# Attention layers of a graph network on one core: projection and maxima in one block instead of two

## What is computed

```python
def gat_layer(x, W, att_src, att_dst, bias, src, dst, n):
    h = (x @ W).reshape(n, 4, 32)
    a_src = einsum('nhc,hc->nh', h, att_src)
    a_dst = einsum('nhc,hc->nh', h, att_dst)
    e = leaky_relu(a_src[src] + a_dst[dst], 0.2)
    m = segment_max(e, dst, num_segments=n)
    ex = exp(e - m[dst])
    denom = segment_sum(ex, dst, num_segments=n)
    out = segment_sum((ex / denom[dst])[:, :, None] * h[src], dst, num_segments=n)
    return out.reshape(n, 128) + bias

h = elu(gat_layer(h, W1, ...)); h = elu(gat_layer(h, W2, ...))
```

## Time and profile before

| | |
|---|---|
| time, median of 3 runs | 6702.77 us (6701.74 to 6705.58) |
| the profiled execution: time / span of its trace | 6699.18 us / 6697.7 us |
| mean granted TensorE clock | 0.856 of full speed |
| TensorE matmul / weight load busy | 4445.1 us (66%) / 2524.8 us (38%) |
| VectorE busy | 3983.5 us (59%) |
| ScalarE busy | 1573.7 us (23%) |
| GpSimd busy | 1564.2 us (23%) |
| L1372, the maxima, two forms of 100 passes | 342.2 us and 342.1 us |
| L1324, the counts, 2500 passes in two layers | some 270 us of busy time in each layer |
| layer 1, first block to end of maxima | 2715.6 to 3130.7 us |
| layer 2, first block to end of maxima | 3886.5 to 4259.9 us |

### The profile page before, as it was taken

How to read it: one execution, slowest core, us unless ns; L and a number is a source line. 1 busy time by engine, 2 the same in 40 slices (tenths; PEclk the granted TensorE clock), 3 DMA queues, 4 the chain that set the end, 5 groups by cost and what they waited for, 6 DMA issues and landing times. The chain is left out here.

```text
span 6697.7 us, 52624 instructions
## 1 busy us (share of the span) xinstructions
PE 4445.1 (66%) x15996; PEld 2524.8 (38%) x15998; DVE 3983.5 (59%) x4400; ACT 1573.7 (23%) x1840; POOL 1564.2 (23%) x1634
## 2 busy tenths in 40 slices
PE   3501111337999999898888888788879887444443
PEld 1100000024554454687333378433334443333333
DVE  6412122678887786698999979899990111111112
ACT  0000000001579700444455410255540003000000
POOL 1677777100000000000000000000000001777776
PEclk9999999999999999656999965799999998555555
DMA  3001010143468606354333346333326666222222
GB/s 58 6 10 18 10 16 12 27 174 134 121 171 237 184 1 246 98 166 125 115 111 111 115 138 188 101 115 111 112 95 245 245 245 172 52 53 53 53 53 56
DMA packets 624187, 729.35 MB, mean 109 GB/s; under 512 B 96339, under 2 KB 556401, under 8 KB 604703
## 3 DMA queue, kind: packets, MB, share of 16 engines
q1 hardware_dynamic: 571790, 669.98, 32.4%
q0 software_dynamic: 52144, 56.00, 3.5%
HBM read 542.42 MB, written 183.38 MB: 108 GB/s over the span
## 5 line engine op out<-in xcount | busy, mean ns | idle before, releaser
L1080 POOL DMA_INDIRECT ring<-rel_dram,rel_pair x806 | 765.6, 950 | 4709.5 <-POOLq L68 4464.2
L878 PE MATMUL total<-to,from 128*128 128x384 f32 x2816 | 939.4, 492 | 34.3 <-issue 28.5
L1625 PE MATMUL sums<-acc,hw 128*64 128x392 f32 x2144 | 747.5, 504 | 138.0 <-DVE acc L1559 137.6
L1160 PE MATMUL total<-ring,onehot 128*128 128x128 f32 x1612 | 415.3, 439 | 579.0 <-DMA ring<-rel_dram,rel_pair 578.5
L517 POOL DMA_INDIRECT cells_dram<-rec,place x742 | 715.8, 965 | 226.1 <-issue 220.0
L686 PE MATMUL alike<-right,left 18*128 18x512 bf16 x352 | 174.4, 616 | 818.6 <-DVE top L646 662.3
L878 PEld LDWEIGHTS total<-to,from 128*128 128x128 f32 x2816 | 524.0, 190 | 450.0 <-issue 121.7
L1115 DVE TENSOR_SCALAR onehot<-iota,loc_pair 128x128 f32<-128x128 f32 x806 | 179.9, 286 | 814.8 <-PE total L1160 814.8
L1160 PEld LDWEIGHTS total<-ring,onehot 128*128 128x128 f32 x1612 | 357.2, 324 | 636.9 <-issue 636.8
L1625 PEld LDWEIGHTS sums<-acc,hw 128*64 128x64 f32 x2144 | 269.7, 138 | 581.2 <-issue 306.9
L620 DVE CAST lo_i<-rows 128x128 int32<-128x128 f32 x11 | 2.7, 244 | 714.8 <-DMA rows<-cells_dram 714.8
(11 more groups left out here) (341 smaller groups left out, 5977.6 us busy)
## 6 DMA issues: line engine op xcount, KB each, us to landing
strip<-ac_dram SPq DMA_DIRECT2D x100, 1600.0 KB, 6.5
count<-ac_dram SPq DMA_DIRECT2D x200, 784.0 KB, 4.2
ac_dram<-stage SPq DMA_DIRECT2D x625, 192.0 KB, 2.4
lo_row<-lo_dram SPq DMA_DIRECT2D x44, 1024.0 KB, 7.3
h<-ac_dram SPq DMA_DIRECT2D x26, 1600.0 KB, 8.3
acc<-ac_dram SPq DMA_DIRECT2D x24, 1600.0 KB, 8.8
rel_dram<-rows SPq DMA_DIRECT2D x25, 1024.0 KB, 5.4
mask_dram<-mask SPq DMA_DIRECT2D x25, 800.0 KB, 5.6
```

The source lines that it names most:

```text
L878: nc.tensor.matmul(spots[:, at(spot), 0:WIDTH].rearrange("p o n -> p (o n)"), from_[:, n % RING, u, :], to[:, n % RING, u, :, :].rearrange ...
L1080: pool.indirect_dma_start(ring[:, j % SLOTS, :], None, m.rel_dram[:, :], bass.IndirectOffsetOnAxis(ap=m.rel_pair[:, j:j + 1], axis=0)).the ...
L1160: last = nc.tensor.matmul(total[:, at(col, D)], onehot[:, j % U, :], ring[:, j % SLOTS, :], start=False, stop=False, skip_group_check=True)
L1625: last = nc.tensor.matmul(psum[kk * 2 * HC:(kk + 1) * 2 * HC, banks(i) + q, 0:PIECE], hw[:, t, k, :], p[n % 3][:, piece], start=t == 0, st ...
```

## The change

Both blocks of `gat_layer` become one. In it:

- SyncE issues the loads of the weight, the attention vectors and the bias and then, with no meeting of engines between, the counts of tiles 0 and 1 (in layer 2 with their masks).
- TensorE makes the 7 pieces of `hwT` (now through four banks), then the 7 spread pieces of head 0, in layer 1 the transposes of tiles 0 and 1, then the spreads of heads 1 to 3, count(0) and count(1). Only then come the 25 row tiles, four at a time into the one bank `proj`, with a wait for ScalarE's copy ahead of each next four, and the 25 score matmuls into the same bank. Tiles 2 to 24 follow as before.
- ScalarE copies the pieces of `hwT`, makes in layer 1 the marks of tile 0, copies head 0, makes mask 0, marks 1 and mask 1, copies heads 1 to 3, and then the row tiles (7 copies, which VectorE did in 25) and the scores (3 copies). Marks of tile 2 and what follows come after that.
- VectorE takes the maxima of tiles 0 and 1 head by head ((0,0), (1,0), (0,1), (1,1), ...), then tile by tile as before.
- A mask buffer is free when the last pass that reads it is done, by the list `TOPS`: for tile 0 that is the seventh pass.

The diff, cut to its core:

```diff
+    quads = [range(t, min(t + 4, NT)) for t in range(0, NT, 4)]
...
-            psum = ps("proj", [P, 8, 512])
...
-                for t in range(NT):
-                    dve.wait_ge(projected, t + 1)
-                    v.tensor_copy(hw[:, t, :, 0:HC], psum[:, 2 + t % 4, 0:D].rearrange("p (h c) -> p h c", h=HEADS)).then_inc(laid, 1)
...
-                for t in range(NT):
-                    if t >= 4:
-                        pe.wait_ge(laid, t - 3)
-                    nc.tensor.matmul(psum[:, 2 + t % 4, 0:D], m.hT[:, t * P:(t + 1) * P], w[:, :], start=True, stop=True).then_inc(projected, 1)
...
-        with phase(nc) as (sb, ps, sem, block_):
...
+            psum, sums, proj = ps("rows", [P, 4, 512]), ps("sums", [P, 512]), ps("proj", [P, 512])
...
+            TOPS = [(T, k) for k in range(HEADS) for T in range(2)] + [(T, k) for T in range(2, NT) for k in range(HEADS)]
...
                     if not first:
                         if T >= 2:
-                            sp.wait_ge(topped, HEADS * (T - 1))
+                            sp.wait_ge(topped, tops_until(T - 2))
...
+                sp.dma_start(w[:, :], weight).then_inc(w_in, 16)
...
                 load(0)
                 load(1)
...
+                pe.wait_ge(kept, len(blocks))
+                pe.wait_ge(ready, 1)
+                spread_head(0)
+                if first:
+                    turn_tile(0)
+                    turn_tile(1)
+                for k in range(1, HEADS):
+                    spread_head(k)
+                count_tile(0)
+                count_tile(1)
+                for g, tiles in enumerate(quads):
+                    if g >= 1:
+                        pe.wait_ge(laid, g)
+                    for c, t in enumerate(tiles):
+                        last = nc.tensor.matmul(proj[:, c * P:(c + 1) * P], m.hT[:, t * P:(t + 1) * P], w[:, :], start=True, stop=True)
+                    last.then_inc(projected, 1)
+                pe.wait_ge(laid, len(quads))
+                for t in range(NT):
+                    last = nc.tensor.matmul(proj[:, t * 8:t * 8 + 8], hwT[:, t * P:(t + 1) * P], att_h[:, :, :].rearrange("p k h -> p (k h)"),
+                                            start=True, stop=True)
+                last.then_inc(scored, 1)
+                for T in range(2, NT):
+                    if first:
+                        turn_tile(T)
+                    count_tile(T)
...
+                if first:
+                    mark(0)
+                keep_head(0)
+                if first:
+                    mask_tile(0)
+                    mark(1)
+                    mask_tile(1)
+                for k in range(1, HEADS):
+                    keep_head(k)
+                for g, tiles in enumerate(quads):
+                    act.wait_ge(projected, g + 1)
+                    n = len(tiles)
+                    nc.scalar.activation(hw[:, tiles[0]:tiles[0] + n, :, 0:HC], proj[:, 0:n * P].rearrange("p (t h c) -> p t h c", t=n, h=HEADS),
+                                         ACT.Copy).then_inc(laid, 1)
+                act.wait_ge(scored, 1)
...
+                if first:
+                    mark(2)
+                    for T in range(2, NT):
+                        mask_tile(T)
                         if T + 1 < NT:
                             mark(T + 1)
...
+                for i, (T, k) in enumerate(TOPS):
```

More of the change, by code:

```diff
@@ L1269, in gat_layer @@
             mask_in, col_in, out = ([sem(f"{n}{k}") for k in range(2)] for n in ("mask_in", "col_in", "out"))
-            ready, marked, turned, counted = (sem(n) for n in ("ready", "marked", "turned", "counted"))
-            d_ = sem("d")
+            w_in, att_in, d_, ready, done, kept, projected, laid, scored, noted = (
+                sem(n) for n in ("w_in", "att_in", "d", "ready", "done", "kept", "projected", "laid", "scored", "noted"))
+            marked, turned, counted = (sem(n) for n in ("marked", "turned", "counted"))
             block = block_()
-            pieces = [(k, cols) for k in range(HEADS) for cols in blocks]
             SPAN = 5
@@ L1305, in _, with spread_head, turn_tile, count_tile @@
             def _(pe):
[L1306 to L1321, removed]
+                def spread_head(k):
+                    for b, cols in enumerate(blocks):
+                        q = len(blocks) * k + b
+                        if q >= 4:
+                            pe.wait_ge(taken, q - 3)
+                        nc.tensor.matmul(psum[:, q % 4, 0:cols.stop - cols.start], att_rep[:, 0, k, :], hwT[:, cols], start=True, stop=True).then_inc(spread, 1)
+                def turn_tile(T):
+                    pe.wait_ge(marked, T + 1)
+                    for s in range(STEPS):
+                        n = T * STEPS + s
+                        if n >= 2:
+                            pe.wait_ge(masked, n - 1)
+                        for q in range(SPAN):
+                            t = s * SPAN + q
+                            last = nc.tensor.transpose(turn[n % 2][:, q * P:(q + 1) * P], there[:, T % 2, t * P:(t + 1) * P], ident_b[:, :])
+                        last.then_inc(turned, 1)
+                def count_tile(T):
                     pe.wait_ge(col_in[T % 2], 16 * (T // 2 + 1))
@@ L1337, in mark, with mask_tile @@
                     nc.scalar.activation(there[:, T % 2, :], cols_of[T % 2].rearrange("p t d -> p (t d)"), ACT.Sign).then_inc(marked, 1)
+                def mask_tile(T):
+                    if T >= 2:
+                        act.wait_ge(topped, tops_until(T - 2))
+                        act.wait_ge(out[T % 2], 16 * (T // 2))
+                    for s in range(STEPS):
+                        n = T * STEPS + s
+                        act.wait_ge(turned, n + 1)
+                        nc.scalar.activation(mask[T % 2][:, s * SPAN * P:(s + 1) * SPAN * P], turn[n % 2][:, 0:SPAN * P], ACT.Identity,
+                                             bias=minus[:, 0:1], scale=BIG).then_inc(masked, 1)
+                for k, cols in enumerate(blocks):
+                    act.wait_ge(done, k + 1)
+                    nc.scalar.activation(hwT[:, cols], psum[:, k % 4, 0:cols.stop - cols.start], ACT.Copy).then_inc(kept, 1)
                 act.wait_ge(ready, 1)
@@ L1341, in _ @@
                     mark(0)
[L1342 to L1351, removed]
+                keep_head(0)
[11 more added lines that the diff above has]
+                act.wait_ge(scored, 1)
+                scores = proj[:, 0:NT * 8].rearrange("p (t k h) -> p t k h", k=2, h=HEADS)
+                nc.scalar.activation(a_src[:, 1, :, :], scores[:, :, 0, :], ACT.Copy, scale=0.2)
+                nc.scalar.activation(a_src[:, 0, :, :], scores[:, :, 0, :], ACT.Copy, scale=0.8)
+                nc.scalar.activation(a_dst[:, :, :], scores[:, :, 1, :], ACT.Copy).then_inc(noted, 1)
+                if first:
+                    mark(2)
+                    for T in range(2, NT):
+                        mask_tile(T)
                         if T + 1 < NT:
```

86 lines of the change are left out of this document (35 added, 51 removed).

## The result

The changed kernel takes 6724.94 us (median of 7 runs, 6719.81 to 6729.02) against 6701.74 us for the kernel before on the same chips (7 runs, 6696.57 to 6707.31): **+23.2 us**, a ratio of 1.0035 with a 95% interval of 1.0024 to 1.0047. The forecast was +26.6 us, 6729.4 us on the median, in a range of 6717 to 6740 us.

What follows compares the result with a forecast made beforehand. The prediction took TensorE to bound layer 1's maxima and VectorE layer 2's unless TensorE falls behind. Layer 1's 17.8 and layer 2's 8.8 summed to +26.6 us, 6729.4 us on the median, range 6717 to 6740 us.

Steps and rivals of the forecast that it cites:

- The bound: Maxima: TensorE sets layer 1's period at 14.4 us a tile; VectorE bounds layer 2 at 13.4 unless TensorE falls behind.
- First maxima: Layer 1, VectorE: the maxima start at 2738.2 in place of 2770.9 on the old trace's clock.
- The sum, +17.8: Layer 1: mask 2 done at 2817.4 in place of 2799.6, +17.8 us, none of it coming back.
- The waits of 6 and 23 us: Layer 2, VectorE: 6 us idle for mask 2, some 23 us idle before tile 4.
- +8.8: Layer 2: tile 4 starts at 3986.7 in place of 3977.9, a delay of 8.8 us that stays.
- The price of the row tiles: TensorE, both layers: 2.76 us a group, 17.7 us in all, read from L1152 at a clock of 0.50.
- the two counts ahead: Row tiles on TensorE: two counts come ahead and lose the high clock level; an argument against the first rival.
- the first rival: TensorE at 2.4 GHz for row tiles and scores: 9.3 us less in each layer, 6711 us; chance 8%.
- the second, faster one: TensorE at 2.4 GHz through the counts too, early start of the maxima kept: 6666 us; chance 2%.
- the slower rival: Layer 1's counts land 5 us later, spreads and count(0) run at the low level: 6740 us; chance 8%.
- The upper end of the range: Whole kernel: unknown sizes, such as later counts and a dearer count(0), taken together give +37 us.
- Copies into `hw`: ScalarE's later copy with stepped output, shown by no row: taken as 0.60 us, as for 512 plain columns.

Runs made afterwards that it cites:

- e1: Changed kernel with row tiles and scores ahead of count(0) and count(1) in both layers; 6714.25 us against 6692.49 before, ratio 1.0030.
- e4: Changed kernel with only 2 of the 25 count matmuls of each tile in layer 1; 6678.15 us against 6699.84 before, ratio 0.9966.
- e5: Kernel before with only 2 of the 25 count matmuls of each tile in layer 1; 6675.70 us against 6699.84 before, ratio 0.9966.
- e7: Changed kernel with layer 1's row tiles straight behind the projection through four banks, layer 2 as in e3; 6677.72 us against 6693.81 before, ratio 0.9974.
- e3: Changed kernel with layer 2's row tiles and scores dealt out behind the counts of later tiles; 6695.62 us against 6692.49 before, ratio 1.0006.
- e2: Changed kernel with row tiles through the four PSUM banks of the spreads, same place; 6691.63 us against 6692.49 before, ratio 0.9997.

## Why the prediction was right

**The bound** was the step on which the sign hung: TensorE in layer 1, in layer 2 VectorE as long as TensorE keeps up. The two runs with few counts show the first, the run with the row tiles spread out the second. The wait table named the right engine where busy shares of 90 and 94% (weight loads and VectorE) could not the earlier trace rows. The rule of the Trainium skill on the highest occupancy (Perfetto Trace Analysis, Identifying the Most-Contended Engine), as the prediction read it, would have had the changed kernel gain; these runs don't agree with it here.

**Layer 1**, by its steps, in us from the section's start. First maxima: forecast 22.6, measured 22.9. Tiles 0 and 1 done: 56.8 and 56.8. count(1) done: 64.9 and 62.9, because count(0) took 5.9 in place of 7.1 and the spreads 17.3 in place of 17.9. Row tiles: 17.7 and 17.7. Scores: 10.8 and 10.8. From there to mask 2: 8.4 and 8.3. Tile 2: 101.8 and 99.8. The sum, +17.8, came out at +15.9.

**Layer 2.** The waits of 6 and 23 us ahead of tiles 2 and 4 were 6.6 and 22.7. The term was +8.8 and measured +10.8: the projection took 8.6 us where I had taken 7.5, and count(0) 8.4 in place of 7.1. Both are a matter of when the level changes. The two layers missed in opposite directions, by 1.9 and 2.0 us; that the sections came to 26.7 us against a sum of 26.6 is luck, and each term is good to 2 us only. Nothing of either delay came back, as forecast.

**The price of the row tiles** was right for these two places, and there was luck in how it was found. I took L1152 at 0.50 as the price of the pattern. Behind the spreads, at the high level, the same groups cost 11.8 us (e1), and behind a few passes of counts 11.9 (e4, layer 1). L1152 itself runs at either level with the same code: groups 2.76 us apart in three of the nine profiles (before, e5, e7) and 1.84 or 1.85 in the other six. In the profile after it even began low; TensorE's clock was 0.50 in the 8 us ahead and rose within the first group:

```profile
5690.00:5698.00 8.00, 2.77 (x6) 0.89 (x7) 3.41 (x17) 0.00 (x0) 2.41 (x3) 0.50 0.55 152
```

```profile
5698.08 1.31 PE L1152 MATMUL total<-w,hT 128*128 128x128 f32 x8 [0.16 <-DMA b_row<-in_L_gnn_b_lin]
5700.07 1.16 PE L1152 MATMUL total<-w,hT 128*128 128x128 f32 x8 [0.69 <-ACT acc L1100]
```

Had the old trace caught it so, the same reading would have given 11.7 us. The better ground was the other one in the prediction, the two counts ahead, which I had named against the first rival. It did not come: groups 2.77 us apart at 0.50 in both layers. Behind two full counts they were so in all four places that the profiles have (both layers of the changed kernel, layer 1 of e3, layer 2 of e4). Nor did the second, faster one: the counts of the middle stretch ran at 0.50 throughout. Of the slower rival one part came, a later landing of the counts (10.1 us in place of 8.1); the first maxima of layer 1 came 0.3 us later than forecast. The upper end of the range has a slip: its terms taken in full (26.6 + 5 + 2 x 3.7) add up to +39 us and not +37. Nothing hung on it.

**Copies into `hw`** with their stepped output took 0.60 us on ScalarE, the value chosen.

## What to carry to other kernels

Before work is moved behind the first steps of a loop, find which engine sets that loop's period, by what ends the waits and not by busy shares: here moved work cost its full length on that engine, and it vanished on another once it was dealt out in portions that fit the slack of an iteration. Moving a part also changes its price. The same 25 matmuls cost here 5.75 us through four banks at the high clock, 7.8 and 8.0 through four banks from the low one, 11.8 through one bank at the high clock and 17.7 through one bank at the low one; so ask what runs just ahead of the new place and how many buffers it has there.

## What the runs showed of the hardware

- **Groups of matmuls with waits between them run at either clock level.** Behind spreads at the high level they kept it: TensorE was busy 7.3 of 11.7 us at 1.00 (e1). Behind two counts they stayed low: 13.2 of 17.5 us at 0.50 (the changed kernel). But L1152 was found at both levels behind the same matmuls, and in the changed kernel's profile and in e2's it rose from the low one in its first group. What decides there no run shows. Through four banks and without waits the same matmuls began at the low level behind two counts and ended at the high one (0.73 on average over 7.5 us, e2). The Trainium skill (TensorE: Matmul & The Clock Gate, Part 1) describes a half-rate level as the default, which activity releases. The row tiles of e2 agree; the counts don't, for with TensorE busy 143.0 of 150 us in the kernel before they ran at 0.50.
- **A busy engine can lose the high level.** In e1 the scores, matmuls of 8 columns back to back with TensorE busy 10.5 of 10.5 us, follow row tiles at 1.00 and run at 0.51. count(0), where it comes straight behind the spreads, gets a few of its passes at the high level: with all its matmuls it took 5.8 to 8.5 us, and the next count 10.8.
- **A small load landed later with large ones issued behind it.** b_row, 64 KB, landed after 4.8 us in place of 2.9 once the counts were issued next in SyncE's queue; in the merged layers of all profiles it was 4.1 to 5.2 us. VectorE's first instruction that needs it started 7.5 us into the section in place of 5.9. (Its wait, 5.6 us in place of 0.8, grew by more, because the fill of `hw`, 2.7 us, now comes behind it.) In the changed kernel:

```profile
b_row<-in_L_gnn_b SPq DMA_DIRECT2D x1, 64.0 KB, 4.8
```

```profile
2725.48 0.49 DVE L1385 TENSOR_SCALAR att_h<-low,att 128x4 f32<-128x4 f32 x2 [5.62 <-DMA b_row<-in_L_gnn_b]
```

  The prediction had left this out. It stayed hidden, since `att_rep` was made at 2727.2 and the spreads could not begin before hwT was copied at 2729.6. No run took it apart, and that the large loads are the cause is not shown.
